# Exponentials of 16 heads at a time in PSUM, products in two halves, and a new sharing of layer 1's rows

## The chip, the cores and the metric

The kernel runs on one core of one Trainium2 chip. The metric is the device time of one execution in microseconds; smaller is better. TensorE multiplies matrices, VectorE and ScalarE do elementwise work and reductions, GpSimd here mostly issues gathers and scatters, and SyncE issues the other transfers. Each engine works off its own list of instructions in order and waits on semaphores for the others.

## What is computed

One block of a transformer: a sparse attention whose neighbours are chosen by a small pairwise network, and a mixture of experts, both on the layer norm of the input, 16 batches of 256 tokens with 256 features. The part that the change touches is the attention:

```python
h = xn @ W1.T                                    # 128 features
pair = relu(h[:, :, None, :] - h[:, None, :, :] + b1)      # layer 1, every pair of tokens
pair = relu(einsum('bijf,gf->bijg', pair, W2) + b2)        # layer 2, 64 features
sim = einsum('bijg,og->bijo', pair, W3)[..., 0] + b3       # layer 3, diagonal set to 0
_, top_idx = top_k(sim, 25)                      # 25 keys for every query
q, k, v = split(xn @ Wqkv.T + bqkv)              # 32 heads of 2 features
scores = q . k / sqrt(2), only at top_idx
out = x + (softmax(scores) @ v) @ Wout.T + bout
```

All is fp32. The pairwise network has 16 x 256 x 256 pairs and is most of the work.

## The kernel before

**The pair steps.** A batch is done in `BSTEPS` = 32 steps, each with 8 query tokens; 16 steps (`STEPS`) are called a half here, and steps are counted from 0 to 15 in it. Layer 1 of a step is 8 rows of 128 x 256: VectorE makes the first `dve_rows(s)` of them (`relu1_row`, L1337), ScalarE the others (`relu1`, L1105). The table in `dve_rows` has 16 entries with the sum 74, so ScalarE makes 54 of 128. Then TensorE does layer 2 of the step (`layer2`, L913, 4 matmuls that the trace shows as 8 records), ScalarE evicts it with bias and relu (`relu2`, L1142, 1024 elements), and after every second step TensorE does layer 3 (`layer3`, L925).

**What ties the engines.** `r1` has 4 buffers, so both makers of rows wait for the product of four steps before (`l2_done`). PSUM holds 3 steps of layer 2 (`PS2`), so the product of step n waits for the eviction of step n-3. ScalarE's program is: rows of step n, then the eviction of step n-3 (`LAG`), and so on without end. VectorE does not evict; between its rows stand, at fixed steps, the operations of the scores, the top-k and the attention of earlier batches (`pair_batch`).

**The attention of a tile** (128 queries; two tiles in a batch, 32 in all) goes as follows. VectorE finds the top 25 of a row in four rounds (steps 6 to 9) and writes the indices at step 10. GpSimd gathers keys and values of 25 rows, one indirect transfer each (`gather_tile`, L742), paced by `l2_done`. In the next half VectorE multiplies queries and keys (step 12, `weigh`, L1493), adds pairs (step 13, L1500), takes the maximum (step 14, L1504) and subtracts it (step 15, L1508). ScalarE takes the exponentials of all 32 heads, 800 elements, after its eviction in step 0 of the half that follows (`exp_scores`, L1146) into the SBUF tile `pexp`. VectorE multiplies them with the values (step 3, `times_values`, L1513, 1600 elements), sums the products (step 4, `sum_values`, L1520), sums the weights (step 10, `sum_weights`, L1525), and divides (step 11). The count of `attn_step` orders these; a tile has `AS` = 9 of them. The query and the maximum of a tile stand in PSUM bank 7, which layer 2 and 3 don't use. The last 4 tiles come later, in the stage of the experts, with their parts placed by tables (`ATTENTION_AT`, `ATTENTION_SLOT`) and their query and maximum in SBUF.

**Around it.** Batches 0 and 1 have no attention yet. GpSimd scatters tokens for the experts in batches 0 and 1, with memsets between as a pause (`rest`, L690), and starts the first gather after that. After the last pair step come the experts and a shared network, bound by matmuls (L953).

Of the kernel before, what the change touches and what calls it, by code (L numbers as in the profile page):

```python
# [5 lines left out]
def lsn_attention_moe_block(  # L6
# [81 lines left out]
    with ctx:  # L88
# [196 lines left out]

        ps_query = ps[:, 7, 0:KD]
        ps_smax = ps[:, 7, KD:KD + HEADS]

# [116 lines left out]
        SUBBED, PV_DONE = 4, 5  # L405
# [12 lines left out]
        def dve_rows(s):  # L418

            return (6, 7, 6, 3, 3, 7, 5, 4, 5, 2, 7, 6, 2, 2, 3, 6)[s % STEPS]  # L420


# [19 lines left out]
        EXP_AT = 0  # L442
# [392 lines left out]
        def _(pe):  # L835
# [121 lines left out]
            def transpose_slots(g):  # L957

                if g == 0:

                    pe.wait_ge(attn_step, (NT - 5) * AS + SUBBED)
# [117 lines left out]
        def _(act):  # L1079
# [64 lines left out]
            def exp_scores(t):  # L1144
                act.wait_ge(attn_step, t * AS + SUBBED)
                nc.scalar.activation(pexp, sc, ACT.Exp, scale=SCALE).then_inc(exp_ready, 1)  # L1146

            for b in range(NB):
                for s in range(BSTEPS):
# [8 lines left out]
                    if s % STEPS == EXP_AT and b > 1:  # L1158
                        exp_scores(b * HALVES + (s // STEPS - 4))
# [62 lines left out]
            for g in range(ALL):  # L1222
# [15 lines left out]
                if g in EXP_GROUP:  # L1238
                    exp_scores(EXP_GROUP[g])
# [23 lines left out]
            for q in range(SLOTS_S):  # L1263
# [12 lines left out]
                if q in EXP_SLOT:  # L1276
                    exp_scores(EXP_SLOT[q])
# [4 lines left out]
        def _(dve):  # L1282
# [228 lines left out]
            def times_values(t, h):  # L1511
                dve.wait_ge(exp_ready, t + 1)
                nc.vector.tensor_tensor(pv.rearrange("p h r d -> p r h d"),  # L1513
                                        kvg[:, h, :, KD:2 * KD].rearrange("p r (h d) -> p r h d", d=2),
                                        pexp.rearrange("p h r -> p r h").unsqueeze(3).to_broadcast([P, TOPK, HEADS, 2]), ALU.mult)\
                    .then_inc(attn_step, 1)

# [4 lines left out]

            def sum_weights(t):
                dve.wait_ge(exp_ready, t + 1)
                nc.vector.tensor_reduce(sums[:, KD:KD + HEADS], pexp, AX, ALU.add).then_inc(attn_step, 1)  # L1525
# [13 lines left out]
            def pair_batch(b, done):  # L1539
# [3 lines left out]
                for s in range(0 if done else ROWS_AHEAD, BSTEPS):  # L1543
# [9 lines left out]
                    for k in range(dve_rows(s)):  # L1553
                        relu1_row(b, s, k)
                        if k == 0:
# [8 lines left out]
                            if late and s16 == 3:  # L1564
                                times_values(summed, h)
                            if late and s16 == 4:
                                sum_values(summed)
                            if late and s16 == 10:
                                sum_weights(summed)
# [74 lines left out]
            def last_attention(t, i):  # L1644
# [9 lines left out]
                if i == 4:  # L1654
                    times_values(t, h)
                if i == 5:
                    sum_values(t)
# [137 lines left out]
```

## Time and profile before

| | us |
|---|---|
| three runs | 1784.99, 1785.21, 1786.67 |
| median | 1785.21 |
| the profiled execution | 1784.96 |
| its span, first to last instruction | 1783.2 |

The mean granted TensorE clock of the profiled execution is 0.995 of full speed. In the profile PE is TensorE's matmuls, DVE is VectorE, ACT is ScalarE, POOL is GpSimd. L1337 is line 1337 of the kernel. "remote" or "another core or an unknown queue" as a releaser means that the profile found nobody whose signal came at that moment; only one core runs. "issue" is time in which nothing that the profile shows was waited for. Ends of matmuls are modelled, and a few of their records can be missing.

Matmuls of layer 2 begin at 95.75 us and the last one at 1402.13; the pair steps lie between, and before them are layer norms and projections.

### The profile page before, as it was taken

Reading aid. Unit: us, or ns where it says so; the run is one execution under the profiler, and the core shown is the slowest. Engines: PE = TensorE matmul, PEld = TensorE weight load, DVE = VectorE, ACT = ScalarE, POOL = GpSimd, SP = SyncE. Lnnn points to the kernel's source line nnn. Section 1 sums busy time; section 2 is a strip of 40 time slices with the busy share of each in tenths; the row PEclk is TensorE's granted clock in tenths of the full one; section 3 lists DMA queues with packets and bytes.
Section 4 is the critical chain, followed back from the end, with each engine's and each line's share of the span. In section 5 each row is a group of like instructions: output and inputs, shape, how many; then the busy total and the mean of one; then the engine's idle time right before and its main releaser. Section 6 shows DMA issues by size and latency. Waiting matters only on the chain.

```text
span 1783.2 us, 30110 instructions
## 1 busy us (share of the span) xinstructions
PE 1656.8 (93%) x9092; PEld 725.2 (41%) x9092; DVE 1499.7 (84%) x4122; ACT 1490.2 (84%) x2772; POOL 1058.5 (59%) x1027
## 2 busy tenths in 40 slices
PE   7999969999999999999999999999999999998998
PEld 6732212222222222222222222222222599997887
DVE  6898948898888889888988988888989588857887
ACT  5699959999999999999999999999999787843342
POOL 3207766666666666666666666666665533455556
PEclk9999989999999999999999999999999999999999
DMA  5722111111111111111111111111131266532333
GB/s 186 249 86 78 56 52 44 47 43 50 44 46 48 45 48 44 49 41 50 43 50 42 50 49 42 50 43 47 44 94 35 63 194 208 170 125 71 119 119 106
DMA packets 80069, 136.84 MB, mean 77 GB/s; under 512 B 22336, under 2 KB 46528, under 8 KB 79936
## 3 DMA queue, kind: packets, MB, share of 16 engines
q0 software_dynamic: 31744, 69.27, 14.3%
q1 hardware_dynamic: 48192, 65.91, 11.3%
q8 instruction: 70, 1.15, 0.3%
q14 instruction: 63, 0.52, 0.1%
HBM read 95.24 MB, written 39.85 MB: 76 GB/s over the span
## 4 chain that ended last, share of the span: by engine, by line
ACT 55%; PE 30%; issue 7%; another core or an unknown queue 3%; DVE 3%; DMA 1%; SPq 1%; POOL 1%; POOLq 0%; ACTq 0%; DVEq 0%
ACT arena L1105 31%; ACT arena L1142 22%; PE ps L913 13%; PE ps L953 10%; PE ps L925 3%; PE ps L877 1%; PE ps L871 1%; PE ps L973 1%; ACT arena L1114 1%; DVE arena L1337 1%; PE ps L844 0%; ACT xT L1091 0%; DMA arena<-xn_rows 0%; DVE hTs_low L1702 0%
## 5 line engine op out<-in xcount | busy, mean ns | idle before, releaser
L742 POOL DMA_INDIRECT arena<-kv_rows,gidx x800 | 823.5, 1029 | 503.1 <-issue 215.4
L913 PE MATMUL ps<-arena,w2t 128*64 128x512 f32 x4096 | 973.3, 601 | 86.6 <-ACT arena L1142 49.8
L1337 DVE TENSOR_SCALAR arena<-arena 128x256 f32<-128x256 f32 x2368 | 759.2, 380 | 158.3 <-PE ps L913 110.5
L1105 ACT ACTIVATE arena<-arena 128x256 f32<-128x256 f32 x1728 | 747.7, 511 | 0.6 <-PE ps L877 0.6
L1142 ACT ACTIVATE arena<-ps,b 128x1024 f32<-128x1024 f32 x512 | 569.7, 1113 | 81.0 <-remote 55.4
L913 PEld LDWEIGHTS ps<-arena,w2t 128*64 128x64 f32 x4096 | 285.0, 136 | 769.0 <-issue 672.4
L925 PE MATMUL ps<-arena,w3win 128*32 128x512 f32 x2048 | 275.9, 605 | 4.6 <-issue 4.5
L925 PEld LDWEIGHTS ps<-arena,w3win 128*32 128x32 f32 x2048 | 41.0, 108 | 212.4 <-issue 170.7
L823 POOL DMA_INDIRECT arena<-slot_outputs,slot_get x64 | 70.0, 1094 | 29.1 <-issue 15.8
L695 POOL DMA_INDIRECT slot_inputs<-arena,slot_put x36 | 40.1, 1114 | 63.3 <-issue 48.1
L1252 ACT ACTIVATE off_diag<-ps 128x512 f32<-128x512 f32 (+1 forms) x24 | 14.3, 595 | 75.8 <-PE ps L953 35.9
L953 PE MATMUL ps<-xTe_high,wug_high 128*112 128x256 f32 (+1 forms) x240 | 70.5, 294 | 0.0
L953 PE MATMUL ps<-xT_high,swug_high 128*128 128x512 f32 x176 | 70.2, 399 | 0.2 <-DVE off_diag L1696 0.2
L953 PE MATMUL ps<-xT_low,swug_high 128*128 128x512 f32 x176 | 69.5, 395 | 0.0
L953 PE MATMUL ps<-xT_high,swug_low 128*128 128x512 f32 x176 | 69.4, 394 | 0.0
L953 PE MATMUL ps<-xTe_low,wug_high 128*112 128x256 f32 (+1 forms) x240 | 67.5, 281 | 0.0
L953 PE MATMUL ps<-xTe_high,wug_low 128*112 128x256 f32 (+1 forms) x240 | 67.3, 280 | 0.0
L953 PE MATMUL ps<-swdn_high,hTs_high 128*128 128x256 f32 x192 | 54.8, 285 | 6.9 <-DVE arena L1726 4.8
L671 POOL TENSOR_TENSOR arena<-arena 128x2 f32<-128x2 f32 x32 | 24.1, 768 | 61.4 <-DVE arena L1301 61.4
L1513 DVE TENSOR_TENSOR arena<-arena 128x1600 f32<-128x1600 f32 x32 | 58.9, 1841 | 0.1
L1520 DVE TENSOR_REDUCE arena<-arena 128x64 f32<-128x1600 f32 x32 | 57.8, 1807 | 0.0
L1252 ACT ACTIVATE xstage<-ps 128x512 f32<-128x512 f32 x24 | 14.4, 598 | 50.3 <-PE ps L953 49.5
(157 smaller groups left out, 1992.5 us busy)
## 6 DMA issues: line engine op xcount, KB each, us to landing
arena<-kv_rows,gidx POOLq DMA_INDIRECT x800
slot_inputs<-arena SPq DMA_DIRECT2D x16, 640.0 KB, 3.9
arena<-slot_inputs SPq DMA_DIRECT2D x40, 256.0 KB
slot_outputs<-arena SPq DMA_DIRECT2D x40, 256.0 KB
arena<-in_L_attn_x_dram SPq DMA_DIRECT2D x16, 256.0 KB, 3.0
xn_rows<-arena SPq DMA_DIRECT2D x16, 256.0 KB, 3.9
arena<-in_L_attn_x_dram SPq DMA_DIRECT2D x8, 512.0 KB
arena<-xn_rows SPq DMA_DIRECT2D x8, 512.0 KB
```

Source lines behind the costliest of these rows:

```text
L695: pool.indirect_dma_start(out=slot_dram, out_offset=bass.IndirectOffsetOnAxis(ap=slots, axis=0), in_=rows, in_offset=None, bounds_check=SL ...
L742: pool.indirect_dma_start(out=kvg[:, h, r, :], out_offset=None, in_=kv_dram, in_offset=bass.IndirectOffsetOnAxis(ap=gidx[:, h, r:r + 1], a ...
L823: pool.indirect_dma_start(out=ys[c % 2][:, n, k, :], out_offset=None, in_=yslot_dram, in_offset=bass.IndirectOffsetOnAxis(ap=slot_get[:, c ...
L913: last = nc.tensor.matmul(ps_l2(n)[v * G2:(v + 1) * G2, u, :], w2t[:, :], r1[:, n % R1, 4 * u + 2 * v:4 * u + 2 * v + 2, :], start=True, s ...
L925: last = nc.tensor.matmul(ps[32 * c:32 * c + 32, 6, :], w3win[:, at:at + 32], r2[:, (2 * q + c // 2) % R2, 512 * (c % 2):512 * (c % 2) + 512],
L953: mm = nc.tensor.matmul(to, weights[a], moving[b], start=(first and i == 0), stop=(last_one and i == 2))
L1105: last = nc.scalar.activation(r1[:, n % R1, k, :], h_rows(b, 0), ACT.Relu, bias=h_rows(b, 1)[:, at:at + 1])
L1142: nc.scalar.activation(r2[:, n % R2, :].rearrange("p (u n) -> p u n", u=2), ps_l2(n), ACT.Relu, bias=b2[:, 0:1]).then_inc(r2_done, 1)
L1252: nc.scalar.activation(sgs[q % 2][rows], ps[:, 2 * (q % 2), :] if m < JC else ps[0:TAIL, 2, :], ACT.Silu).then_inc(ssilu_done, 1)
L1337: row = nc.vector.tensor_scalar(r1[:, (b * BSTEPS + s) % R1, k, :], h_rows(b, 0), h_rows(b, 1)[:, at:at + 1], 0.0, ALU.add, ALU.max)
L1513: nc.vector.tensor_tensor(pv.rearrange("p h r d -> p r h d"), kvg[:, h, :, KD:2 * KD].rearrange("p r (h d) -> p r h d", d=2), pexp.rearran ...
L1520: nc.vector.tensor_reduce(sums[:, 0:KD].rearrange("p (h d) -> p h d", d=2), pv.rearrange("p h r d -> p h d r"), AX, ALU.add)\
```

## The change

1. The table of `dve_rows` is replaced; its sum is 81 instead of 74.
2. The exponentials are taken in two parts of 16 heads (`PART`), 400 elements each. For the first 28 tiles both parts go, one after the other, into the same place in PSUM bank 7 (`ps_exp`, behind query and maximum); for the last 4 into `pexp` as before. ScalarE takes part 0 after its eviction in step 0, part 1 after that in step 4. Part 1 overwrites part 0, so it waits until VectorE has used part 0 (`SUBBED + 2`).
3. VectorE multiplies and sums in two parts: product and sum of the weights of part 0 in step 3, product of part 1 in step 6, sum of its weights in step 7. The sum of the products goes from step 4 to step 10. In the last 4 tiles the parts follow each other in the groups 4 and 5 of the tables.
4. `PV_DONE` is 7 instead of 5 and `AS` 11 instead of 9, so GpSimd's gather into the place of a tile waits for the product of part 1. TensorE's first transpose of the experts, which uses bank 7, waits for the last use of `ps_exp`.

The core of the diff:

```diff
+        PART = HEADS // 2
+        ps_exp = ps[:, 7, KD + HEADS:KD + HEADS + PART * TOPK].rearrange("p (h r) -> p h r", r=TOPK)
-        SUBBED, PV_DONE = 4, 5
+        SUBBED, PV_DONE = 4, 7
-            return (6, 7, 6, 3, 3, 7, 5, 4, 5, 2, 7, 6, 2, 2, 3, 6)[s % STEPS]
+            return (7, 7, 7, 3, 7, 7, 2, 3, 5, 6, 3, 7, 2, 5, 5, 5)[s % STEPS]
+        def exps(t, part):
+            return ps_exp if t < NT - 4 else pexp[:, part * PART:(part + 1) * PART, :]
-        EXP_AT = 0
+        EXP_AT = (0, 4)
-                    pe.wait_ge(attn_step, (NT - 5) * AS + SUBBED)
+                    pe.wait_ge(attn_step, (NT - 5) * AS + (PV_DONE + 1))
-            def exp_scores(t):
-                act.wait_ge(attn_step, t * AS + SUBBED)
-                nc.scalar.activation(pexp, sc, ACT.Exp, scale=SCALE).then_inc(exp_ready, 1)
+            def exp_scores(t, part):
+                act.wait_ge(attn_step, t * AS + (SUBBED if part == 0 or t >= NT - 4 else SUBBED + 2))
+                nc.scalar.activation(exps(t, part), sc[:, part * PART:(part + 1) * PART, :], ACT.Exp, scale=SCALE).then_inc(exp_ready, 1)
-                    if s % STEPS == EXP_AT and b > 1:
-                        exp_scores(b * HALVES + (s // STEPS - 4))
+                    if s % STEPS in EXP_AT and b > 1:
+                        exp_scores(b * HALVES + (s // STEPS - 4), EXP_AT.index(s % STEPS))
-            def times_values(t, h):
-                dve.wait_ge(exp_ready, t + 1)
-                nc.vector.tensor_tensor(pv.rearrange("p h r d -> p r h d"),
-                                        kvg[:, h, :, KD:2 * KD].rearrange("p r (h d) -> p r h d", d=2),
-                                        pexp.rearrange("p h r -> p r h").unsqueeze(3).to_broadcast([P, TOPK, HEADS, 2]), ALU.mult)\
+            def times_values(t, h, part):
+                heads, cols = slice(part * PART, (part + 1) * PART), slice(KD + part * 2 * PART, KD + (part + 1) * 2 * PART)
+                dve.wait_ge(exp_ready, 2 * t + part + 1)
+                nc.vector.tensor_tensor(pv[:, heads, :, :].rearrange("p h r d -> p r h d"),
+                                        kvg[:, h, :, cols].rearrange("p r (h d) -> p r h d", d=2),
+                                        exps(t, part).rearrange("p h r -> p r h").unsqueeze(3).to_broadcast([P, TOPK, PART, 2]), ALU.mult)\
                     .then_inc(attn_step, 1)
+            def sum_weights(t, part):
+                dve.wait_ge(exp_ready, 2 * t + part + 1)
+                nc.vector.tensor_reduce(sums[:, KD + part * PART:KD + (part + 1) * PART], exps(t, part), AX, ALU.add).then_inc(attn_step, 1)
                             if late and s16 == 3:
-                                times_values(summed, h)
-                            if late and s16 == 4:
+                                times_values(summed, h, 0)
+                                sum_weights(summed, 0)
+                            if late and s16 == 6:
+                                times_values(summed, h, 1)
+                            if late and s16 == 7:
+                                sum_weights(summed, 1)
+                            if late and s16 == 10:
                                 sum_values(summed)
-                            if late and s16 == 10:
-                                sum_weights(summed)
```

**VectorE, steps 3 to 6 of a half with attention.** L1337 is a row of layer 1; a row that waits for `l2_done` is the first of its step. Before:

```order
L1337 TENSOR_SCALAR arena<-arena 128x256 [waits l2_done]
L1513 TENSOR_TENSOR arena<-arena 128x25x32x2 [waits exp_ready]
L1337 TENSOR_SCALAR arena<-arena 128x256 x2
L1337 TENSOR_SCALAR arena<-arena 128x256 [waits l2_done]
L1520 TENSOR_REDUCE arena<-arena 128x64 [waits attn_step]
L1337 TENSOR_SCALAR arena<-arena 128x256 x2
L1337 TENSOR_SCALAR arena<-arena 128x256 [waits l2_done]
L1337 TENSOR_SCALAR arena<-arena 128x256 x6
```

In the changed kernel, steps 3 to 6, where L1346 is the row of layer 1, L1523 the product, L1530 the sum of the weights, L1460 the score operation and L1468 the first of the top-k:

```order
L1346 TENSOR_SCALAR arena<-arena 128x256 [waits l2_done]
L1523 TENSOR_TENSOR arena<-arena,ps 128x25x16x2 [waits exp_ready]
L1530 TENSOR_REDUCE arena<-ps 128x16 [waits exp_ready]
L1346 TENSOR_SCALAR arena<-arena 128x256 x2
L1346 TENSOR_SCALAR arena<-arena 128x256 [waits l2_done]
L1346 TENSOR_SCALAR arena<-arena 128x256 x6
L1346 TENSOR_SCALAR arena<-arena 128x256 [waits l2_done]
L1460 SCALAR_TENSOR_TENSOR arena<-ps,b,off_diag 128x512 [waits l3_done]
L1346 TENSOR_SCALAR arena<-arena 128x256 x6
L1346 TENSOR_SCALAR arena<-arena 128x256 [waits l2_done]
L1468 MAX top<-arena 128x8 [waits sim_taken]
L1523 TENSOR_TENSOR arena<-arena,ps 128x25x16x2 [waits exp_ready]
```

The product of 25 x 32 x 2 elements from SBUF has become one of 25 x 16 x 2 from PSUM with the weights' sum behind it, the long sum of the products is gone from here, and step 4 has seven rows instead of three.

**ScalarE, from step 0.** L1105 is a row, L1142 an eviction, L1146 the exponential. Before, from the eviction of step 0 to the first row of step 4:

```order
L1142 ACTIVATE arena<-ps,b 128x1024 [waits l2_done]
L1146 ACTIVATE arena<-arena 128x800 [waits attn_step]
L1105 ACTIVATE arena<-arena 128x256 [waits l2_done]
L1142 ACTIVATE arena<-ps,b 128x1024 [waits l2_done]
L1105 ACTIVATE arena<-arena 128x256 [waits l2_done]
L1105 ACTIVATE arena<-arena 128x256
L1142 ACTIVATE arena<-ps,b 128x1024 [waits l2_done]
L1105 ACTIVATE arena<-arena 128x256 [waits l2_done]
L1105 ACTIVATE arena<-arena 128x256 x4
L1142 ACTIVATE arena<-ps,b 128x1024 [waits l2_done]
L1105 ACTIVATE arena<-arena 128x256 [waits l2_done]
```

In the changed kernel, steps 0 to 4, with L1111, L1148 and L1153 in their places:

```order
L1148 ACTIVATE arena<-ps,b 128x1024 [waits l2_done]
L1153 ACTIVATE ps<-arena 128x400 [waits attn_step]
L1111 ACTIVATE arena<-arena 128x256 [waits l2_done]
L1148 ACTIVATE arena<-ps,b 128x1024 [waits l2_done]
L1111 ACTIVATE arena<-arena 128x256 [waits l2_done]
L1148 ACTIVATE arena<-ps,b 128x1024 [waits l2_done]
L1111 ACTIVATE arena<-arena 128x256 [waits l2_done]
L1111 ACTIVATE arena<-arena 128x256 x4
L1148 ACTIVATE arena<-ps,b 128x1024 [waits l2_done]
L1111 ACTIVATE arena<-arena 128x256 [waits l2_done]
L1148 ACTIVATE arena<-ps,b 128x1024 [waits l2_done]
L1153 ACTIVATE ps<-arena 128x400 [waits attn_step]
```

The exponential of 800 elements in SBUF is two of 400 in PSUM, the second behind the eviction in step 4 and with a wait for VectorE's `attn_step`, and steps 2 and 4 have one row instead of two and five.

## Rows read from the trace of the kernel before

Steps are those of a half. In 560 to 1330 us every half has the same work, but for the score operation, which occurs in every second one.

**Rows 1.** Page of the profile, part 1: busy us (share of the span) xinstructions, by engine.

```profile
PE 1656.8 (93%) x9092; PEld 725.2 (41%) x9092; DVE 1499.7 (84%) x4122; ACT 1490.2 (84%) x2772; POOL 1058.5 (59%) x1027
```

**Rows 2.** Timeline, VectorE: start us, us, engine, line, operation; the score operation, batches 2 and 15.

```profile
276.71 0.75 DVE L1451 SCALAR_TENSOR_TENSOR arena<-ps,b,off_diag 128x512 f32<-128x512 f32 x1
...
1332.74 0.74 DVE L1451 SCALAR_TENSOR_TENSOR arena<-ps,b,off_diag 128x512 f32<-128x512 f32 x1
```

**Rows 3.** Windows view, 560 to 1330 us: busy us of PE, PEld, DVE, ACT, POOL; clock.

```profile
560.00:1330.00 770.00, 722.24 (x3644) 193.58 (x3638) 678.84 (x1967) 730.00 (x1347) 504.65 (x493) 1.00 0.18 49
```

**Rows 4.** Chain that ended last, in order of time: start us, us, what.

```profile
199.34 3.58 PE ps L913 x16
202.93 1.00 PE ps L925 x8
```

**Rows 5.** Waits, 560 to 1330 us: waiting engine and line, waited for: us, times, longest.

```profile
DVE arena L1337 <- PE ps L913: 71.8, 38, 2.4
...
PE ps L913 <- ACT arena L1142: 33.1, 57, 1.1
ACT arena L1142 <- remote: 30.2, 19, 1.7
...
DVE arena L1493 <- DMA arena<-kv_rows,gidx: 1.2, 5, 0.3
```

**Rows 6.** The chain again, around 977 us.

```profile
976.17 1.65 another core or an unknown queue
...
978.95 2.39 ACT arena L1105 x6
```

**Rows 7.** Timeline of all engines, in brackets the idle time before a row and its releaser.

```profile
971.79 3.65 PE L913 MATMUL ps<-arena,w2t 128*64 128x512 f32 x16
...
976.37 1.08 PE L913 MATMUL ps<-arena,w2t 128*64 128x512 f32 x4
...
977.84 1.11 ACT L1142 ACTIVATE arena<-ps,b 128x1024 f32<-128x1024 f32 x1 [1.67 <-remote]
977.84 0.35 DVE L1337 TENSOR_SCALAR arena<-arena 128x256 f32<-128x256 f32 x1 [1.43 <-remote]
```

**Rows 8.** Timeline of VectorE, rows of layer 1 around 960 us.

```profile
952.34 7.34 DVE L1337 TENSOR_SCALAR arena<-arena 128x256 f32<-128x256 f32 x24
961.69 0.35 DVE L1337 TENSOR_SCALAR arena<-arena 128x256 f32<-128x256 f32 x1 [2.00 <-PE ps L913]
```

**Rows 9.** Groups by line, 560 to 1330 us: shapes xcount | busy us, mean ns | idle.

```profile
L1105 ACT ACTIVATE arena<-arena 128x256 f32<-128x256 f32 x1025 | 442.3, 507 | 0.0
L1337 DVE TENSOR_SCALAR arena<-arena 128x256 f32<-128x256 f32 x1406 | 441.9, 372 | 89.3 <-PE ps L913 71.8 <-remote 17.5
...
L1513 DVE TENSOR_TENSOR arena<-arena 128x1600 f32<-128x1600 f32 x19 | 34.9, 1838 | 0.0
...
L1466 DVE FIND_INDEX8 idx<-top,arena 128x8 uint32<-128x256 f32 x76 | 31.5, 414 | 0.0
...
L1525 DVE TENSOR_REDUCE arena<-arena 128x32 f32<-128x800 f32 x19 | 18.6, 980 | 0.0
L1508 DVE TENSOR_TENSOR arena<-arena,ps 128x800 f32<-128x800 f32 x19 | 18.5, 975 | 0.0
L1146 ACT ACTIVATE arena<-arena 128x800 f32<-128x800 f32 x19 | 16.8, 885 | 0.0
```

**Rows 10.** Groups by line, whole span: a reduction of 256 elements.

```profile
L1425 DVE TENSOR_REDUCE arena<-arena 128x32 f32<-128x256 f32 x2 | 0.8, 420 | 0.1
```

**Rows 11.** Timeline of VectorE, batches 0 and 1.

```profile
192.81 24.60 DVE L1337 TENSOR_SCALAR arena<-arena 128x256 f32<-128x256 f32 x58
...
251.71 2.19 DVE L1337 TENSOR_SCALAR arena<-arena 128x256 f32<-128x256 f32 x8 [9.22 <-remote]
```

**Rows 12.** Timeline of GpSimd: issues of two gathers.

```profile
962.48 2.15 POOL L742 DMA_INDIRECT arena<-kv_rows,gidx  x1 [2.43 <-PE ps L913]
964.93 0.95 POOL L742 DMA_INDIRECT arena<-kv_rows,gidx  x1 [0.30 <-issue]
```

More of the change, by code:

```diff
@@ L1238, in _ @@
                 if g in EXP_GROUP:
-                    exp_scores(EXP_GROUP[g])
+                    for part in range(2):
+                        exp_scores(EXP_GROUP[g], part)
                 if g == TOKENS_HIGH:
@@ L1276, in _ @@
                 if q in EXP_SLOT:
-                    exp_scores(EXP_SLOT[q])
+                    for part in range(2):
+                        exp_scores(EXP_SLOT[q], part)
             slot_high(SLOTS_S - 1)
@@ L1521, in sum_values @@
                     .then_inc(attn_step, 1)
-            def sum_weights(t):
-                dve.wait_ge(exp_ready, t + 1)
-                nc.vector.tensor_reduce(sums[:, KD:KD + HEADS], pexp, AX, ALU.add).then_inc(attn_step, 1)
             def invert(t):
@@ L1654, in last_attention @@
                 if i == 4:
-                    times_values(t, h)
+                    times_values(t, h, 0)
+                    sum_weights(t, 0)
                 if i == 5:
+                    times_values(t, h, 1)
+                    sum_weights(t, 1)
+                if i == 6:
                     sum_values(t)
-                if i == 6:
-                    sum_weights(t)
                 if i == 7:
```

## The prediction

> **What bounds the kernel now.** I read the page first: TensorE is busy 93% of the span, VectorE and ScalarE 84% each [rows 1]. That names no bound, because matmul ends are modelled and several stages are averaged. So I looked at one stage. From batch 2 on the pair steps, 32 for each batch, carry the attention beside them, and the change touches little else. I call 16 steps a half. The operation that takes the scores of a batch occurs once in 32 steps: at 276.71 in batch 2 and at 1332.74 in batch 15, 26 halves apart [rows 2]. A half therefore lasts 1056.03 / 26 = 40.62 us, and 26 halves make 1056 of the 1783 us.
>
> The busy times over 560 to 1330 us [rows 3] are 18.96 halves: VectorE 678.84 / 18.96 = 35.81 us a half, ScalarE 730.00 / 18.96 = 38.51 us. TensorE never runs below its floor: two steps of layer 2 take 3.58 us and one group of layer 3 takes 1.00 us [rows 4], so a half needs 8 x 4.58 = 36.64 us. ScalarE is thus the fullest, with 2.11 us idle, nearly all of it in one wait of up to 1.7 us in each half [rows 5]. The chain of waits says the same: ScalarE's rows and evictions, one wait, then ScalarE again [rows 6]. VectorE idles 4.81 us a half, in three waits for TensorE [rows 5]. **ScalarE's work plus 2.1 us of waiting sets the 40.62 us.**
>
> These waits are odd, and everything below depends on them. At 977.84 both ScalarE (eviction of step 5) and VectorE (rows of step 9) start after idling, and both wait for the product of step 5. By the records this was the first half of the x16 that began at 971.79 and ended near 973.6. They are released only while the product of step 7 runs (started 976.37) [rows 7]. I take from this, as a pattern I can't explain, that the signal of step 5 becomes visible 1.47 us after the start of step 7's product. The same happens at step 3 (VectorE starts at 961.69 after 2.00 us idle [rows 8]) and at step 14. Check of the pattern: TensorE works without a break of any size from step 4's product to step 7's, 7.4 us, and then 1.5 us more, 8.9 in all; ScalarE meanwhile has 11 rows (0.398 each, 2.39 for six [rows 6]) and 3 evictions of 1.0, 7.4 us. The difference is 1.5 us; the row shows 1.67 [rows 7].
>
> **The change, part by part.**
>
> 1. Rows of layer 1: VectorE's table sums to 74 before and 81 after, so 7 rows a half go from ScalarE to VectorE. VectorE does 24 in 7.34 us, 0.304 for each further one [rows 8]: +2.13 us. ScalarE loses 7 x 0.398 = 2.79 us.
>
> 2. Exponentials: one of 800 elements, 885 ns, becomes two of 400. A row of 256 takes 507 ns [rows 9], so an element costs 0.69 ns and 400 take 0.61 us. Neighbours overlap by 0.11 (0.507 against 0.398), so two cost 1.00 where one cost 0.77: ScalarE +0.23 us.
>
> 3. Products with the values: one of 1600 elements, 1838 ns, becomes two of 800. The row of 800 elements with one operand in PSUM takes 975 ns [rows 9]. Records on VectorE overlap by 0.07 (a row reads 0.372 [rows 9] and adds 0.304), so 2 x 0.91 against 1.77: +0.05 us. Bounds: 0 (the start hides) and +1.8 (each half as dear as a whole, since no row reads PSUM with a stride of 25 elements). I take 0.05, from the 975 ns of a row that reads PSUM.
>
> 4. Sums of the weights: 980 ns becomes two of 400. A reduction of 256 takes 420 ns [rows 10], so 400 take 0.57: +0.09 us. Bounds 0 and +0.98.
>
> Sum for VectorE: 35.81 + 2.13 + 0.05 + 0.09 = **38.08 us a half**. ScalarE: 38.51 - 2.79 + 0.23 = 35.95. TensorE 36.64, plus 0.91 because step 8's product needs step 5's eviction, which follows the late release (977.84 + 1.11 + 0.12 against 976.37 + 1.79): 37.55. VectorE becomes the fullest.
>
> 5. Can it be full? Once per late release. Step 3: it is released about 2.3 us after VectorE ends step 0; steps 1 and 2 (14 rows) last 4.26. Step 9: 1.6 to 1.8 us after step 7; step 8 (5 rows, 1.5 us, and three top-k operations like the 414 ns one [rows 9], at least 1.0) lasts 2.5. Step 14: 1.1 us after step 12; step 13 (5 rows, 0.91 of adding pairs) lasts 2.4. All three have over 1 us of room, where they had none because ScalarE held TensorE back. ScalarE's stretch from step 4 to step 8 now holds 15 rows, three evictions and half an exponential, 9.5 us against TensorE's 8.9, so its wait disappears; step by step it ends before VectorE, by the least (under 0.1 us) at step 8.
>
> 6. The new wait: ScalarE's second exponential, after its eviction in step 4, waits for VectorE's product and sum of step 3. Queued behind it are ScalarE's row of step 5 (one) and the eviction of step 2. VectorE is there 0.30 + 0.91 + 0.50 us into step 3; the product of step 5 can then start 2.1 us later, and VectorE ends its own rows of step 5 over 4 us later. Covered; without cover it would cost up to 1 us a half. VectorE's second product, in step 6, has two steps of 7 rows ahead of it. The gather into the tile's place now waits until step 6 instead of 3, but it also waits for indices of step 10.
>
> I add 0.5 us a half for jitter between engines now within 2 us of each other: 38.6. Stage: 26 x (40.62 - 38.6) = 53 us. Batch 15 after its scores has fewer operations on VectorE, so it goes from ScalarE's pace to TensorE's: 3 to 4 us. Before batch 2 I count nothing, within 3 us each way: there VectorE's rows beside GpSimd's memsets cost 24.60 / 58 = 0.42 us, which makes 7 more dear, and all engines then stop for up to 9.22 us at 251.71 [rows 11] while the first gathers run, which swallows lead. The expert stage has 4 of the 32 tiles, off TensorE's path. Sum: 1785 - 57 = **1728 us**. The profiled execution took 1784.96 us (span 1783.2, 1.8 around it), the median is 1785.21, so no correction.
>
> **A rule of the skill.** A gather's issue takes 2.15 us where VectorE runs its product of two SBUF operands (962.48), and 0.95 beside VectorE's rows, as at 964.93 [rows 12]. The Trainium skill (SBUF — State Buffer, "SBUF: two separate sides") says that VectorE holds a port pair shared with GpSimd in two-port modes, one-source fp32 operations among them, and GpSimd then can't write descriptors. By that rule the 7 more rows speak against this change.
>
> **Rivals.**
>
> - **Half the gain.** The late releases move with the denser program, or VectorE catches the pattern at two of its three places, 0.7 us each: 38.1 + 1.4 = 39.5, 26 x 1.1 = 29, with 4 at the end: 1752 us. For it: I don't know what causes them. The same time follows if PSUM with a stride costs half its bound in parts 3 and 4 (1.4 us).
> - **Slower: the idle stays.** If VectorE's 4.81 us of idle belongs to TensorE's timetable and not to ScalarE's pace, the new work lands on top. It decides from 40.62 - 38.08 = 2.54 us of idle that stays. With three quarters (3.6): 41.7 a half, 26 x 1.1 = 28 more, 1813 us; with all, 1844. For it: VectorE waits for TensorE at the same three steps in every half. Against: TensorE has 4 us of slack a half and waits for ScalarE's evictions (33.1 us [rows 5]).
> - **GpSimd late.** If each of the 7 rows holds the gathers up by its 0.30 us, they land 2.1 us later. VectorE already waits for them in 5 of 19 halves, by 0.3 at most [rows 5]: 40.2 a half, 1774 us. By that port rule it would be so; the 0.95 us beside rows speaks against it.
> - **No change** (1782 to 1789): what stays idle is just the 2.5 us.
> - **Better than the sum**: no jitter and fewer holds between GpSimd and VectorE, 38.0: 1713 us.
>
> **How the numbers follow.** Forecast (1716 to 1742) 0.58; half the gain (1742 to 1768) 0.16; GpSimd late 0.03; better 0.04; no change 0.06; slower 0.13. Likeliest time 1728. Range 1714 to 1770: both first cases and most of the bounds of parts 3 and 4 (all of them, +2.7 us, would be 1797, which I count with the slower case). A difference under 0.2% (3.6 us) can't be told from none. Faster 0.58 + 0.16 + 0.03 + 0.04 = 0.81, same 0.06, slower 0.13.
>
> **What would show it.** Spacing of the score operation: 26 halves in about 1004 us. VectorE busy near 98%, its waits for TensorE under 1 us a half; ScalarE busy near 36 us with more idle; half products near 0.98 us, half sums near 0.57, half exponentials near 0.61. I am wrong if VectorE still idles over 2 us a half, if a half product costs over 1.2 us, or if ScalarE's second exponential waits with TensorE idle behind it.

## The result, and the profile after

The changed kernel takes 1763.88 us (median of four runs, 1763.39 to 1768.34) against 1785.1 us of the kernel before beside it: a ratio of 0.9883, 95% interval 0.987 to 0.9897. It is faster by 21 us, in the range, but the forecast was 57 us. The profiled execution took 1763.39 us (span 1761.7).

Start with the spacing of the score operation. Timeline of VectorE, batches 2 and 15, to be held against [rows 2]:

```profile
283.18 0.75 DVE L1460 SCALAR_TENSOR_TENSOR arena<-ps,b,off_diag 128x512 f32<-128x512 f32 x1 [2.49 <-remote]
...
1315.42 0.74 DVE L1460 SCALAR_TENSOR_TENSOR arena<-ps,b,off_diag 128x512 f32<-128x512 f32 x1
```

26 halves take 1032.24 us, 39.70 us each; before 40.62, forecast 38.6. So 560 to 1330 us are 19.40 halves. Windows view of that stretch (busy us of PE, PEld, DVE, ACT, POOL; clock), beside [rows 3]:

```profile
560.00:1330.00 770.00, 732.47 (x3722) 198.04 (x3721) 734.01 (x2187) 695.01 (x1265) 500.85 (x504) 1.00 0.19 50
```

VectorE is busy 37.84 us a half (forecast 38.08), ScalarE 35.83 (forecast 35.95). The work is as I summed it. What is wrong is the idle time: 1.86 us a half on VectorE, 3.87 on ScalarE. Groups by line, the operations whose prices I estimated, beside [rows 9]:

```profile
L1346 DVE TENSOR_SCALAR arena<-arena 128x256 f32<-128x256 f32 x1564 | 483.0, 372 | 36.0 <-PE ps L919 22.4 <-remote 11.8
...
L1523 DVE TENSOR_TENSOR arena<-arena,ps 128x800 f32<-128x800 f32 x39 | 37.9, 973 | 0.0
...
L1530 DVE TENSOR_REDUCE arena<-ps 128x16 f32<-128x400 f32 x39 | 21.8, 559 | 0.0
L1153 ACT ACTIVATE ps<-arena 128x400 f32<-128x400 f32 x39 | 19.4, 498 | 0.0
```

Products (973 ns) and sums (559) cost what was forecast, the exponentials less (498 instead of 610), and none of them waits. Who waits, in the waits view of the same stretch (us in total, times, longest), beside [rows 5]:

```profile
ACT arena L1148 <- PE ps L919: 47.2, 12, 4.0
PE ps L919 <- ACT arena L1148: 31.4, 48, 1.4
ACT arena L1148 <- remote: 27.5, 9, 3.9
...
DVE arena L1346 <- PE ps L919: 22.4, 22, 1.7
DVE arena L1346 <- remote: 11.8, 13, 1.5
```

ScalarE's one long wait a half, which my forecast had removed, is now longer (up to 4.0 us, before 1.7). The timeline of all engines shows it at step 3 of the half that starts at 948.3:

```profile
946.51 3.65 PE L919 MATMUL ps<-arena,w2t 128*64 128x512 f32 x16
...
950.45 0.95 POOL L748 DMA_INDIRECT arena<-kv_rows,gidx  x1 [0.30 <-issue]
951.09 0.20 PEld L919 LDWEIGHTS ps<-arena,w2t 128*64 128x64 f32 x4 [0.84 <-issue]
951.09 1.94 PE L919 MATMUL ps<-arena,w2t 128*64 128x512 f32 x8
...
953.01 1.11 ACT L1148 ACTIVATE arena<-ps,b 128x1024 f32<-128x1024 f32 x1 [3.89 <-PE ps L919]
953.01 0.35 DVE L1346 TENSOR_SCALAR arena<-arena 128x256 f32<-128x256 f32 x1 [1.50 <-PE ps L919]
...
953.80 0.95 POOL L748 DMA_INDIRECT arena<-kv_rows,gidx  x1 [2.40 <-PE ps L919]
...
954.27 1.08 PE L919 MATMUL ps<-arena,w2t 128*64 128x512 f32 x4 [1.24 <-ACT arena L1148]
```

The eviction of step 15 waits for the first eight of the sixteen records that begin at 946.51; by the records they end near 948.3. ScalarE, VectorE and GpSimd go on together at 953.0 to 953.8, 4.7 us later. TensorE has done steps 0 and 1 meanwhile and then waits itself, for that eviction. GpSimd had issued ten gathers in a row, the last one ending at 951.40. It is so in all 19 halves of the stretch: ScalarE and VectorE go on 1.5 to 1.8 us after the last of ten gathers. In the kernel before, their waits of over 1.2 us end 0.8 to 2.0 us after a gather too, nearly always the last of eight or ten. That alone doesn't tell which causes which, since GpSimd waits for the same signals; this is where the experiments begin.

Before batch 2 the kernel lost: its first product there starts at 272.7, before at 269.2. From there to batch 15 it gains 22.2 us, and 2.8 in batch 15.

### The profile page after: what moved, and what is told of

Its sections match the earlier page's. It is cut to its first block, busy times and chain, and to the rows that moved or that the text cites. A ratio compares the mean times of both kernels' runs of the same rounds, so it can differ in the third digit from the quotient of the medians.

```text
span 1761.7 us, 30206 instructions
## 1 busy us (share of the span) xinstructions
PE 1655.0 (94%) x9092; PEld 725.3 (41%) x9092; DVE 1565.8 (89%) x4410; ACT 1404.6 (80%) x2580; POOL 1039.1 (59%) x1027
## 4 chain that ended last, share of the span: by engine, by line
ACT 41%; PE 34%; issue 6%; DVE 6%; another core or an unknown queue 5%; DMA 1%; SPq 1%; POOL 1%; POOLq 0%; DVEq 0%; ACTq 0%
ACT arena L1111 21%; PE ps L919 19%; ACT arena L1148 18%; PE ps L959 9%; PE ps L931 5%; DVE arena L1346 3%; ACT ps L1153 1%; PE ps L979 1%; DMA arena<-xn_rows 0%; DVE hTs_low L1717 0%; POOL arena L829 0%; DMA arena<-slot_inputs 0%; DVE xTe_low L1626 0%; DVE hTe_low L1637 0%
## 5 line engine op out<-in xcount | busy, mean ns | idle before, releaser
L748 POOL DMA_INDIRECT arena<-kv_rows,gidx x800 | 794.5, 993 | 496.7 <-issue 225.8
L1346 DVE TENSOR_SCALAR arena<-arena 128x256 f32<-128x256 f32 x2592 | 817.1, 379 | 77.4 <-remote 41.2
L1148 ACT ACTIVATE arena<-ps,b 128x1024 f32<-128x1024 f32 x512 | 567.1, 1108 | 144.5 <-PE ps L919 72.9
L1111 ACT ACTIVATE arena<-arena 128x256 f32<-128x256 f32 x1504 | 655.4, 508 | 0.6 <-PE ps L883 0.6
L701 POOL DMA_INDIRECT slot_inputs<-arena,slot_put x36 | 44.2, 1228 | 65.9 <-issue 50.7
L959 PE MATMUL ps<-swdn_low,hTs_high 128*128 128x256 f32 x192 | 55.0, 286 | 0.3 <-issue 0.3
L959 PE MATMUL ps<-swdn_high,hTs_low 128*128 128x256 f32 x192 | 54.9, 286 | 0.0
```

Source lines behind the costliest of these rows:

```text
L701: pool.indirect_dma_start(out=slot_dram, out_offset=bass.IndirectOffsetOnAxis(ap=slots, axis=0), in_=rows, in_offset=None, bounds_check=SL ...
L748: pool.indirect_dma_start(out=kvg[:, h, r, :], out_offset=None, in_=kv_dram, in_offset=bass.IndirectOffsetOnAxis(ap=gidx[:, h, r:r + 1], a ...
L959: mm = nc.tensor.matmul(to, weights[a], moving[b], start=(first and i == 0), stop=(last_one and i == 2))
L1111: last = nc.scalar.activation(r1[:, n % R1, k, :], h_rows(b, 0), ACT.Relu, bias=h_rows(b, 1)[:, at:at + 1])
L1148: nc.scalar.activation(r2[:, n % R2, :].rearrange("p (u n) -> p u n", u=2), ps_l2(n), ACT.Relu, bias=b2[:, 0:1]).then_inc(r2_done, 1)
L1346: row = nc.vector.tensor_scalar(r1[:, (b * BSTEPS + s) % R1, k, :], h_rows(b, 0), h_rows(b, 1)[:, at:at + 1], 0.0, ALU.add, ALU.max)
```

## The experiments

Theories at the start. **P**: the late signals hang on a place in TensorE's program (what my prediction assumed: "the signal of step 5 becomes visible 1.47 us after the start of step 7's product"). **G**: they come from GpSimd's gathers. All kernels of a set ran on one chip, beside the kernel before, which took 1797.0, 1785.1, 1704.4, 1797.5 and 1784.4 us in the five sets. That spread is a finding of its own, below. "Half" is the mean of 15 halves from batch 5 to batch 12, from the starts of layer 2's products.

### Set 1: each part alone, and another pace

Rows alone on the kernel before; the changed kernel with the old rows:

```diff
-            return (6, 7, 6, 3, 3, 7, 5, 4, 5, 2, 7, 6, 2, 2, 3, 6)[s % STEPS]
+            return (7, 7, 7, 3, 7, 7, 2, 3, 5, 6, 3, 7, 2, 5, 5, 5)[s % STEPS]
```

> The kernel before with the new table of rows alone (81 of 128 on VectorE); exponentials, products and sums stay whole and in their old places. Theory (the step that failed is the one on the late releases: they stop both engines, however the attention is cut): nearly all of the measured gain comes from the rows, 1764 to 1770 us, a half 39.7 to 40.0, VectorE busy 37.9 a half. Rival (the gain hangs on the halves, since a product of 1.8 us and the sum of products of 1.8 us in steps 3 and 4 now stand before seven rows each and hold TensorE back): 1780 to 1800 us, a half over 40.6.

Measured: 1800.1 us, ratio 1.0022 (1.0004 to 1.004), a half 40.93. The theory fell: the rows alone give nothing. ScalarE has 2.7 us less to do in each half (35.8) and idles 5.1: its evictions of the steps 5, 10 (or 6) and 15 all wait for a signal that comes 4.2 to 5.3 us, in the mean of each step, after the last record of the product has begun. The rival has the right number; whether for its reason, set 5 shows.

> The changed kernel with the old table of rows (74 of 128 on VectorE); exponentials in two parts in PSUM, products in halves. Theory (ScalarE's work and its wait set the pace again): ScalarE busy 35.83 + 2.79 = 38.6 a half, a half 40.6 to 40.9, 1783 to 1792 us. Rival (the parts by themselves free TensorE earlier): under 1780 us.

Measured: 1791.9 us, ratio 0.9979 (0.9965 to 0.9993), a half 40.58, as the theory had it. Each part alone changes the time by 0.2%, in opposite directions; both together bring 1.2%. Terms that add up don't do that.

Then the pace of GpSimd, with the same gathers:

```diff
-                    wait_alone(pool, "pool", l2_done, b * BSTEPS + (BSTEPS + GATHER_AT + op * BSTEPS // ROW))
+                    wait_alone(pool, "pool", r2_done, b * BSTEPS + (BSTEPS + GATHER_AT - 3 + op * BSTEPS // ROW))
```

> The changed kernel with GpSimd's gathers and scatters paced by ScalarE's count of evictions (three steps less) in place of TensorE's count of products; the same gathers, at nearly the same times. Theory G in the form that GpSimd and the late signal feed each other (GpSimd waits for the same late signal, then issues a burst of 8 to 10 gathers, which makes the next signal late): the bursts shift with ScalarE's evictions, and the steps at which VectorE and ScalarE wait move or the waits shrink; 1735 to 1760 us. Theory P: the same steps and lengths of waits, 1760 to 1766 us.

Measured: 1901.5 us, ratio 1.0575 (1.0547 to 1.0604). Both missed the size, but P is out: nothing changed in TensorE's program, and the waits moved to other steps and grew to 7.1 us; the half is 45.01. Timelines of ScalarE, of TensorE and of GpSimd, where GpSimd issued twelve gathers without a rest (the first at 1051.84, the last ending at 1066.64):

```profile
1059.71 1.11 ACT L1148 ACTIVATE arena<-ps,b 128x1024 f32<-128x1024 f32 x1 [0.34 <-PE ps L919]
1060.72 2.10 ACT L1111 ACTIVATE arena<-arena 128x256 f32<-128x256 f32 x5
1068.96 1.12 ACT L1148 ACTIVATE arena<-ps,b 128x1024 f32<-128x1024 f32 x1 [6.14 <-remote]
```

```profile
1059.94 3.65 PE L919 MATMUL ps<-arena,w2t 128*64 128x512 f32 x16
1063.52 1.78 PE L931 MATMUL ps<-arena,w3win 128*32 128x512 f32 x3
1066.81 0.59 PE L931 MATMUL ps<-arena,w3win 128*32 128x512 f32 x1 [1.51 <-issue]
1068.21 2.63 PE L931 MATMUL ps<-arena,w3win 128*32 128x512 f32 x4 [0.81 <-issue]
1070.77 2.61 PE L919 MATMUL ps<-arena,w2t 128*64 128x512 f32 x8
```

```profile
1065.69 0.95 POOL L748 DMA_INDIRECT arena<-kv_rows,gidx  x1 [0.31 <-issue]
```

The eviction at 1068.96 is that of step 4, whose last record began at 1058.42, 10.5 us earlier; it goes on 2.3 us after the last gather of the run (1.6 us in the changed kernel, 951.40 to 953.01). And TensorE itself stands still: eight matmuls of layer 3, which need 1.07 us elsewhere, take from 1063.52 to 1070.8, with nothing to wait for ("issue"). A lower clock is not the reason: up to 1068.9 each record has its usual 0.6 us, and only the ones after it are longer (1.05 us; the mean granted clock from 1063 to 1071 us is 0.86). The kernel's own pacing by TensorE's count hides how bad this is: GpSimd waits for the same late signal, and so each run of gathers ends after eight or ten.

### Set 2: thinner and fewer gathers

A memset of 16 or 128 columns ahead of each paced gather:

```diff
+                        nc.gpsimd.memset(idle_cols[:, 0:128], 0.0).then_inc(paused, 1)
```

> The changed kernel with a memset of 16 columns on GpSimd ahead of each paced gather. A gather then starts about 1.4 to 1.5 us after the one before instead of 1.25. Theory G (a run of gathers without pause makes the signals of TensorE's products visible late): the runs are thinner, the 2.4 us pauses of GpSimd and the waits of VectorE (1.5 us) and ScalarE (3.9 us) at step 3 shrink; before batch 2 the stop of all engines in the first gathers shrinks as well; 1735 to 1758 us. Theory P (the place in TensorE's program): the same waits, 1760 to 1766 us. If it is the number of gathers in flight and not their spacing, no change either.

Measured: 1797.7 us, ratio 1.0075 (1.0046 to 1.0103). It tells nothing of spacing: a gather still follows the last after 1.26 us, since the memset fits into the 0.3 us between them. The half is 41.17, and ScalarE waits over 0.3 us at eight of the sixteen steps, though not at all of them in each half: a small shift of the gathers costs 34 us.

> The same with a memset of 128 columns: 1.5 to 1.65 us from gather to gather, 26 in a half take 39 to 43 us, so GpSimd itself may become the fullest. Theory G: the late signals vanish, VectorE and ScalarE wait for gathers instead; 1740 to 1800 us, with the stop in the first gathers gone. Theory P: the waits at the same steps stay and the gathers come on top, over 1790 us.

Measured: 1777.3 us, ratio 0.9953 (0.9936 to 0.997); 1.46 us from gather to gather, a half 40.57. The late signals did not vanish (evictions start up to 9.5 us after a product), so a spacing of 1.46 instead of 1.26 us is no cure.

Gathers left out (a form that thinned the first two tiles as well gave no time, since their attention would have read rows that nothing had written):

```diff
-                for r in rows:
+                for r in (rows if paced != TOPK or first else range(1)):
```

> The changed kernel with one gather instead of 25 for tiles 2 to 27; the other 24 rows of these tiles are left out and hold what the first two tiles gathered. Theory G: no release later than 1 us after the end of the product, the waits of VectorE at step 3 (1.5 us) and of ScalarE at step 3 (3.9 us) are gone, a half 38.1 to 38.6 as forecast, 1728 to 1740 us. Theory P: waits at the same steps and of the same length, a half 39.4 to 39.7, 1758 to 1764 us.

Measured: 1683.9 us, ratio 0.9429 (0.9404 to 0.9453). G stands. Windows view, 560 to 1100 us (columns as above):

```profile
560.00:1100.00 540.00, 540.00 (x2836) 143.56 (x2832) 519.99 (x1654) 527.62 (x958) 28.61 (x28) 1.00 0.03 8
```

TensorE is busy 540.00 of 540 us, the half is 36.64, exactly its floor of 8 x 4.58, and where ScalarE still waits it goes on 0.6 us after the last record began. It beat the expectation, because VectorE got lighter too: a row takes 346 ns in place of 372. Groups by line, the same stretch:

```profile
L1346 DVE TENSOR_SCALAR arena<-arena 128x256 f32<-128x256 f32 x1194 | 334.0, 346 | 1.1 <-PE ps L919 1.1
```

> The changed kernel once more, as a base for the others on the same chip: a ratio of 0.987 to 0.990 to the kernel before.

Measured: 1763.8 us, ratio 0.9878 (0.9852 to 0.9903). Its profiled execution was the longest of five, 1775.3 us: most halves take 39.8 us there, and a few up to 49.1.

### Set 3: a chip on which nothing comes late

I sent these to tell bytes from descriptors and to price the change without gathers. The kernel before took 1704.4 us in this set, 80 us and more below the others, and that changed what they tell.

> The kernel before with one gather of 25 for tiles 2 to 27, as in the run of the changed kernel that took 1684 us and 36.66 a half. If the sum of my forecast was right but for the gathers, ScalarE's work alone sets its half: 38.4 to 38.6, 1715 to 1735 us, and the change is worth 1.8 to 2.0 us a half without gathers, as forecast. Rival (the change is worth no more than the measured 0.9 us also without gathers): 37.4 to 37.7, 1700 to 1712 us.

The same edit as above on the kernel before. Measured: 1704.3 us, ratio 1.0001 (0.9992 to 1.0011). Here the gathers cost the kernel before nothing. Windows view, 560 to 1100 us:

```profile
560.00:1100.00 540.00, 519.82 (x2707) 138.92 (x2704) 477.02 (x1458) 540.00 (x1003) 29.40 (x28) 1.00 0.03 8
```

ScalarE is busy 540.00 of 540 us and the half is 38.30: my 38.51 for ScalarE was right, and the 2.1 us on top of it are the late signals. The time is in the range of the rival (1700 to 1712 us) and below that of the theory, the half 0.1 us below the theory's; neither had counted on a chip on which the gathers cost nothing.

```diff
-            EVERY = 1
+            EVERY = 4
```

> The changed kernel; GpSimd waits for TensorE's count only ahead of every fourth gather of a tile, so groups of four (5 us) with a rest of about 1.2 us between, if nothing is late. If the length of a run of gathers makes the signals late, these short runs don't: a half 38 to 39, 1720 to 1750 us. If the gathers themselves do, however grouped: 39.4 to 40, 1758 to 1775 us.

Measured: 1693.1 us, ratio 0.9943 (0.9922 to 0.9964), all gathers in. A half 37.66, below both ranges. Windows view, 560 to 1100 us:

```profile
560.00:1100.00 540.00, 533.27 (x2758) 136.04 (x2756) 538.99 (x1616) 515.16 (x929) 391.10 (x370) 1.00 0.18 49
```

VectorE is busy 538.99 of 540 us: this is the forecast's own picture ("VectorE busy near 98%"), on a chip without late signals. No eviction that waited began more than 0.64 us after the last record of its product, though GpSimd issued over forty gathers in a row several times.

> The changed kernel with GpSimd starting plain transfers of 128 rows of 512 bytes in place of the indirect gathers of tiles 2 to 27: the same bytes, the same number of transfers, at the same paces, but the rows are those of the tile's own tokens and not the chosen ones. Theory I (it is the indirect gathers' own work, the descriptors that GpSimd makes for each row): no late signals, a half 36.7 to 37.5, 1685 to 1710 us. Theory D (it is the bytes or the writes to the buffer): the late signals stay, a half near 39.7, 1750 to 1765 us.

```diff
+                    if paced == TOPK and not first:
+                        pool.dma_start(kvg[:, h, r, :], kv_dram[ds(b * (2 * P) + h * P, P), :]).then_inc(gathered[h], 16)
+                        continue
```

> The changed kernel with 13 gathers of 25 for tiles 2 to 27, the other 12 rows left over from the first tiles. They come in the first 8 of the 16 steps between two tiles, 17 us of gathers and 20 us of rest in a half. If lateness grows with the length of the run of gathers and is gone after a rest, one late signal a half in place of three: a half 37.3 to 38.5, 1700 to 1735 us. If it goes by the number of gathers alone: half of the 3.0 us, 38.2. If any gather at all sets the slower pace: 39.4 or more.

Measured: 1665.95 and 1666.5 us, ratios 0.9776 and 0.9778, halves 36.64 and 36.68. Inconclusive here, since there was no late signal to remove, so both were run again.

### Set 4: the same, where signals come late

> The changed kernel again, to see it beside the others on one chip. Where the kernel before takes 1785 us or more, signals come late: 1762 to 1775 us, a half 39.7 to 40.7. Where it takes 1704 us (a chip on which no signal was late), VectorE alone sets the half: 37.6 to 38.1, 1680 to 1700 us, a ratio of 0.986 to 0.998, since ScalarE's 38.3 of the kernel before is replaced by VectorE's 37.8.

Measured: 1779.2 us (4 us above the range), ratio 0.9896 (0.9879 to 0.9912), a half 40.24, with late evictions of two steps (9 and 15) in every half in place of one.

> The kernel of the run with plain transfers in place of the gathers of tiles 2 to 27. On a chip with late signals: theory I (the descriptors that GpSimd makes for each row) a half 36.7 to 37.5, 1685 to 1710 us, as without gathers; theory D (the bytes) near 39.7, 1750 to 1765. On a chip without late signals: 36.64, about 1666 us, which tells nothing.

Measured: 1686.3 us, ratio 0.9383 (0.9367 to 0.9398). Theory I. Windows view, 560 to 1100 us:

```profile
560.00:1100.00 540.00, 540.00 (x2834) 143.63 (x2832) 519.60 (x1654) 527.79 (x958) 316.75 (x383) 1.00 0.18 51
```

The same bytes in rows of 512, started by GpSimd, and no signal is late in this stretch; TensorE is at its floor. Groups by line, 560 to 1100 us, the changed kernel and then this one:

```profile
L1346 DVE TENSOR_SCALAR arena<-arena 128x256 f32<-128x256 f32 x1081 | 333.9, 371 | 33.0 <-remote 21.1 <-PE ps L919 11.8
L748 POOL DMA_INDIRECT arena<-kv_rows,gidx x334 | 327.9, 982 | 191.1 <-issue 87.2 <-PE ps L919 76.0 <-remote 26.1
```

```profile
L1349 DVE TENSOR_SCALAR arena<-arena 128x256 f32<-128x256 f32 x1194 | 332.9, 342 | 1.4 <-PE ps L922 1.2
L749 POOL DMA_DIRECT2D arena<-kv_rows x369 | 301.9, 821 | 204.2 <-PE ps L922 153.5 <-issue 38.9 <-DVE gidx L1483 6.6
```

It is not the amount of traffic. Two reserves: these 128 rows stand one behind the other in memory where the gathered ones are scattered, so the run doesn't part the index work from the scattered addresses; and GpSimd needs 0.82 us for such a transfer and 0.98 for a gather, and waits for TensorE's count 89 times in these 540 us where the changed kernel does so 42 times, so the runs are shorter too.

> The kernel of the run with 13 gathers of 25. On a chip with late signals: if lateness grows with the length of a run of gathers and is gone after a rest, a half 37.3 to 38.5, 1700 to 1735 us; if any gather sets the slower pace, 39.4 or more. On a chip without late signals: 36.7, about 1666 us.

Measured: 1699.7 us, ratio 0.9455 (0.9432 to 0.9478), a half 37.11, just below the range. The gathers come mostly one to five in a row, with rests of 0.7 to 1.8 us, and then GpSimd rests for half of the steps. ScalarE still finds a late signal nearly once in a half (17 times in the 20.8 halves from 560 to 1330 us, 3.0 us after the last record in the mean, up to 4.9), but there is slack for it: most halves take 36.6 to 36.8 us, some 37.5 and one 39.4.

> The kernel of the run with GpSimd's wait ahead of every fourth gather. On a chip with late signals: if the run of gathers since the last rest makes them late, the forced rest of 1.2 us after four helps: under 1750 us. If the rest is too short or missing after the first late signal: 1758 to 1775 us. On a chip without late signals: as before, ratio 0.994.

Measured: 1814.0 us, ratio 1.008 (1.0053 to 1.0106), a half 41.52. Both ranges missed it. Against the kernel before it gained 11 us on the chip without late signals and loses 17 here. After the first late signal GpSimd is behind its pace, the waits for the next groups are met already, and eight gathers come in a row again, at times twelve.

### Set 5: the parts without gathers, and the early batches

> The kernel before with the new table of rows alone and with one gather of 25 for tiles 2 to 27. With all gathers the rows alone gave nothing (1.0022), the parts alone nothing (0.9979), both together 0.988. If that is because the late signals fall at other steps, without gathers the rows alone do all the work: ScalarE 38.3 - 2.8 = 35.5, VectorE 33.9 + 7 x 0.27 = 35.8, TensorE's 36.64 sets the half: 36.6 to 36.9, as in the changed kernel without gathers. Rival (the whole product and sum in steps 3 and 4, beside the rows that the new table puts there, hold TensorE back by themselves): over 37.2.

Measured: 1683.8 us, ratio 0.9441 (0.9425 to 0.9456), a half 36.64. Without gathers the rows alone do all of it: that they gave nothing in set 1 was the late signals' doing, and not the product and sum of VectorE in steps 3 and 4. (VectorE's rows are about 25 ns lighter here, as in every run without gathers, so a small part of the latter can't be excluded.)

> The changed kernel on the same chip, as the base for the one with the old rows early: a ratio of 0.987 to 0.990 to the kernel before on a chip with late signals. On a chip where no signal is late, VectorE sets the half: 37.6 to 38.1, a ratio of 0.986 to 0.998.

Measured: 1765.0 us, ratio 0.9899 (0.9882 to 0.9916), a half 39.76.

```diff
-            return (7, 7, 7, 3, 7, 7, 2, 3, 5, 6, 3, 7, 2, 5, 5, 5)[s % STEPS]
+            return ((6, 7, 6, 3, 3, 7, 5, 4, 5, 2, 7, 6, 2, 2, 3, 6) if b < 2 else (7, 7, 7, 3, 7, 7, 2, 3, 5, 6, 3, 7, 2, 5, 5, 5))[s % STEPS]
```

> The changed kernel with the old table of rows in batches 0 and 1 and the new one from batch 2 on. The trace of the changed kernel enters batch 2 at 272.7 us where that of the kernel before enters it at 269.2, and the kernel with the old table alone at 269.5. If that is the price of the rows there, this kernel is 3 us faster than the changed one on the same chip (0.2%), half the part of the missing gain that lies before batch 2. If it is swallowed by the gathers later, no difference.

Measured: 1762.8 us (1762.0 to 1765.0), ratio 0.9882 (0.9865 to 0.9898), against 1764.6 to 1770.0 of the changed kernel beside it. The first product of batch 2 starts at 269.7 instead of 272.8, so the rows were the cause. But at the second half of batch 3 both are at 391 to 392 us, and the last product starts within 0.2 us: swallowed. The 2 us between the medians come after the pair steps, and I can't say from what. Of the kernels that do the whole work where signals are late it is the fastest by its median, but not by more than the intervals allow. No experiment gave a clear improvement on the changed kernel where signals are late.

## Why the prediction was right in sign and wrong in size

**Bound before: half right.** ScalarE's work and one wait set the 40.62 us, as I read. But I took the wait for slack between the engines, to be closed by giving ScalarE less work. The kernel before without gathers shows the split: 38.30 us of ScalarE's work and 2.3 us of late signals. The changed kernel is split the same way: 37.66 of VectorE's work (set 3, gathers grouped) and 2.1 on top, 39.75. By this estimate the change moved the work by 0.64 us, from 38.30 to 37.66, and left the late signals nearly as they were (2.3 and 2.1): 0.9 us a half, where the forecast had 2.0. The changed kernel itself was not run where nothing is late.

**Parts 1 to 4: right.** VectorE 37.84 for 38.08, ScalarE 35.83 for 35.95, half product 973 ns for 975, half sum 559 for 570; half exponential 498 for 610, mis-sized by 0.11 us each, on an engine with room.

**Part 5: the step that failed.** It asked whether VectorE can be full, and answered from the three places of the late releases, "all three have over 1 us of room", and "its wait disappears". Both took the releases to stay at the places in the half that the old trace showed, tied to TensorE's products as in "1.47 us after the start of step 7's product". They are tied to the end of GpSimd's runs of gathers, and move with them: the release for step 15 was to come 2.3 us after VectorE ends step 0, with 4.26 us of rows to cover it. It came 6.0 us after (VectorE's 21 rows start at 944.74, the first seven of them are step 0 and end near 947.0; the release is at 953.01) and cost VectorE 1.50 and ScalarE 3.89 us. My check of the pattern (1.5 us worked out, 1.67 read) was made on one instance, in the kernel from which the pattern was taken; it could not tell a tie to TensorE from a tie to GpSimd, which waits 2.43 us at 962.48, just behind the late release at 961.69 [rows 8, 12].

**Part 6: right.** No second exponential, product or weighing waits; GpSimd's gathers are not later. The 0.5 us for jitter was meant for this kind of trouble, and is a quarter of it.

**Batch 15 and the start: nearly.** 2.8 us gained for 3 to 4, and 3.5 us lost before batch 2, where I had counted nothing within 3. In set 5 giving the early batches their old rows brought these back there and not at the end.

**The rivals.** "Half the gain" had the mechanism in its first words ("the late releases move with the denser program") and the number: 39.5 us and 1752 forecast, 39.70 and 1763.9 measured. "The idle stays" was right in kind: 1.86 of 4.81 us of VectorE's idle stayed, below the 2.54 from which it decides. I gave the two 0.29 together; for a pattern that I called unexplained and on which "everything below depends", that was too little. The rule on the shared port did not decide: a gather's issue takes 982 ns in the mean, 1025 before.

## What to carry to other kernels

When several engines resume at one moment, long after the record of what they waited for, look at what every other engine did just before that moment, the ones that only start transfers above all, before the pattern is built into a sum. An unexplained wait is not slack: price a change once with it gone and once with it kept, and let the second carry as much weight as the first until something shows the cause. A kernel with its gathers thinned out is a cheap way to read what the other engines can do, and the same kernel before has to be in every set, since its time was 1704 in one and 1784 to 1797 in the others.

## What the runs showed of the hardware

- **Indirect gathers hold TensorE up.** So it was in four of the five sets. Where GpSimd issued them without a rest (1.26 us each), TensorE's signals became visible late: 5.2 us after the product's last record had begun at the end of ten gathers, 10.5 at the end of twelve. In that last place TensorE's own matmuls stopped as well, with nothing to wait for (7.3 us for 1.07 us of work), and went on 1.6 us after the last gather. Plain transfers of the same size from GpSimd did nothing of the kind (36.64 against 40.24 us a half in one set). How the gathers do it is open, and so is whether their scattered addresses have a part in it. The Trainium skill (DMA: Bandwidth & Descriptors, "SWDGE vs HWDGE vs iDMA") says that GpSimd writes the descriptors of both kinds, direct and indirect; by that alone the two should act alike, and here they don't.
- **It is not there always.** In one set of five the kernel before took 1704.4 us, and taking its gathers away changed nothing. There even forty gathers in a row made nothing late, so no length of a run does it by itself. The rest of the kernel differs as well: from the last product of layer 2 to the end it took 370.5 to 372.2 us in the kernels of that set and 377.6 to 381.5 in all others. Two of the sets came from the chip of the same number (1797.0 and 1784.4 us), so the number alone doesn't set the time. What does is open.
- **The records of TensorE don't show it.** The row of the product of step 15 ends near 948.3 in the trace, and three engines see it at 953.0. The Trainium skill (Perfetto Trace Analysis, "Tensor Engine Instruction (MATMUL, LD_WEIGHTS)") says that the end is computed from the size of the instruction and that the signal leaves only when PSUM has acknowledged the writes. The trace agrees, in that the three engines see it 4.7 us after that end.
- **Gathers make VectorE slower as well.** A row of 256 takes 371 ns beside all gathers, 346 with one of 25 and 342 beside plain transfers; at 81 rows 25 ns are 2.0 us a half, and my 38.08 holds them.
